# Local attention: the bound on sums of squares as a pairwise maximum, and new step tables for all engines

## The reference, cut to what matters

```python
qkv = x @ Wqkv                       # 16 heads of 64, after a shift of tokens
q = l2norm(q) * qs ; k = l2norm(k) * ksc   # t / max(norm(t), 1e-12)
q = q * cos * scale + rotate_half(q) * sin * scale     # k alike with 1/scale
sim = einsum('bhwie,bhwje->bhwij', bq, bk2) * 8        # window 32, masked
out = einsum('bhwij,bhwje->bhwie', softmax(sim), bv2)
x = x + out @ Wo
```

## Time and profile before

| | us |
|---|---|
| median of 3 runs | 4976.01 (4972.33 to 4977.17) |
| profiled execution, its own time | 4975.52 |
| its span in the trace | 4973.7 |
| busy in the span: PE, DVE, ACT, POOL | 4338.5, 3926.2, 3584.8, 3207.4 |
| first layer's local attention, first product to last normalisation | 584.0 to 1093.6 |

### The profile page before, as it was taken

How to read it: one execution, slowest core, us unless ns; L and a number is a source line. 1 busy time by engine, 2 the same in 40 slices (tenths; PEclk the granted TensorE clock), 3 DMA queues, 4 the chain that set the end, 5 groups by cost and what they waited for, 6 DMA issues and landing times. The chain is left out here.

```text
span 4973.7 us, 153122 instructions
## 1 busy us (share of the span) xinstructions
PE 4338.5 (87%) x50692; PEld 2786.0 (56%) x50694; DVE 3926.2 (79%) x9246; ACT 3584.8 (72%) x13078; POOL 3207.4 (64%) x4057
## 2 busy tenths in 40 slices
PE   6949899988999889998899979998899986676765
PEld 3426566664666646665466645666466664444533
DVE  4779899965999569994899939997499964777488
ACT  5938688874888558884788838887388864777434
POOL 2512399964999569993799928997399962323163
PEclk8969999999999999999999989999899998888886
DMA  2000000000000000000000000000000000000000
GB/s 57 0 19 0 5 2 0 0 18 6 2 0 0 19 7 1 0 0 19 7 0 0 0 24 2 0 0 2 23 2 0 0 18 1 0 0 0 1 26 18
DMA packets 36456, 34.77 MB, mean 7 GB/s; under 512 B 11590, under 2 KB 31300, under 8 KB 35140
## 3 DMA queue, kind: packets, MB, share of 16 engines
q1 hardware_dynamic: 36164, 31.14, 2.1%
HBM read 29.03 MB, written 2.10 MB: 6 GB/s over the span
## 5 line engine op out<-in xcount | busy, mean ns | idle before, releaser
L2477 ACT ACTIVATE local_prob<-ps,local_shift_by 128x128 f32<-128x128 f32 x3072 | 1080.6, 378 | 8.8 <-DVE local_shift_by L2557 8.7
L2405 POOL TENSOR_TENSOR local_qk<-local_qk,local_rsin 128x512 f32<-128x512 f32 x768 | 968.9, 1272 | 61.1 <-DVE local_rsin L2582 61.0
L2716 PE MATMUL ps<-local_wqkv,local_xsT 128*128 128x512 f32 x1536 | 853.2, 642 | 68.4 <-DVE local_rsin L2582 24.9
L2412 POOL TENSOR_TENSOR local_qk<-local_qk,local_inv 128x512 f32<-128x512 f32 x768 | 793.7, 1045 | 174.3 <-ACT local_inv L2496 174.3
L2419 POOL TENSOR_TENSOR local_prob<-local_prob,local_rs 128x512 f32<-128x512 f32 x768 | 791.5, 1042 | 12.6 <-DVE local_rs L2564 12.6
L2477 ACT ACTIVATION_READ_ACCUMULATOR local_prob<-ps,local_shift_by 128x1 f32 x3072 | 670.8, 218 | 0.0
L2571 DVE TENSOR_TENSOR local_qk<-ps,local_cos_t 128x512 f32<-128x512 f32 x768 | 519.7, 677 | 95.0 <-ACT local_sq L2485 90.3
L2485 ACT ACTIVATE local_sq<-ps 128x512 f32<-128x512 f32 x768 | 464.4, 605 | 155.9 <-PE ps L2716 141.9
L2557 DVE TENSOR_REDUCE local_shift_by<-ps 128x4 f32<-128x512 f32 x768 | 524.4, 683 | 63.1 <-PE ps L2792 54.1
L2582 DVE TENSOR_TENSOR local_rsin<-ps,local_sin_t 128x256 f32<-128x256 f32 x1536 | 570.8, 412 | 0.0
L2589 DVE TENSOR_REDUCE local_ss<-local_sq 128x8 f32<-128x512 f32 x768 | 511.4, 667 | 7.8 <-ACT local_sq L2485 7.8
(11 more groups left out here) (331 smaller groups left out, 9174.0 us busy)
## 6 DMA issues: line engine op xcount, KB each, us to landing
local_wqkv<-L_ffn_Wqkv SPq DMA_DIRECT2D x7, 1536.0 KB, 6.8
local_wo<-L_ffn_Wo SPq DMA_DIRECT2D x7, 512.0 KB, 7.3
out<-quantised_res SPq DMA_DIRECT2D x8, 256.0 KB, 2.3
local_w<-L_ffn_W SPq DMA_DIRECT2D x6, 341.0 KB
L_cross_decay<-c_decay SPq DMA_DIRECT2D x1, 1024.0 KB, 11.8
local_w<-L_ffn_W SPq DMA_DIRECT2D x12, 64.0 KB
load_raw<-L_ffn_w SPq DMA_DIRECT2D x8, 64.0 KB, 2.2
local_b<-L_ffn_b SPq DMA_DIRECT2D x24, 0.5 KB
```

Of the source, the lines that this page charges most:

```text
L2405: nc.gpsimd.tensor_tensor(qk[w][:, j, :, :], qk[w][:, j, :, :], rsin[j % 2][:, :, :], ALU.add).then_inc(rot_ready, 1)
L2412: nc.gpsimd.tensor_tensor(qk[w][:, j, :, :], qk[w][:, j, :, :], bcast(inv[:, w, 8 * j:8 * j + 8].unsqueeze(2), [P, 8, LH]), ALU.mult).then ...
L2477: last = nc.scalar.activation(prob[w][:, g, j, :], ps[:, 4 + g % 2, j * P:(j + 1) * P], ACT.Exp, bias=shift_by[:, w, h:h + 1], accum_out=s ...
L2716: nc.tensor.matmul(proj_bank(j), xsT[w][:, :], wqkv[:, 512 * j:512 * j + 512], start=True, stop=True).then_inc(proj_ready, 1)
```

## The change

The sums of squares get a second column per head that holds the constant 1e-24, written once per layer by POOL. The bound is then a `tensor_reduce` that takes the maximum over each pair and writes a new tile `bounded`, where it was a `tensor_scalar` in place. The logarithm reads `bounded`. The four step tables and the one of PE are rewritten, with other leads and lags. Each engine keeps the same calls: the evacuations of DVE are still `evacuate_qk(…, p = 1)`, values half 0 and heads half 1, the others are still ACT's. No wait inside a function is changed.

```diff
-    ss, lnss, inv = (sb(n, [P, 2, 4 * 8]) for n in ("ss", "lnss", "inv"))
+    ss = sb("ss", [P, 2, 4 * 8, 2])
+    bounded, lnss, inv = (sb(n, [P, 2, 4 * 8]) for n in ("bounded", "lnss", "inv"))
...
+            nc.gpsimd.memset(ss[:, :, :, 1:2], 1e-24)
...
-            sequence_loop(pool, NB, 0, 6, step)
+            sequence_loop(pool, NB, 6, 0, step)
...
-                    nc.scalar.activation(lnss[:, w, :], ss[:, w, :], ACT.Ln, scale=2.0 ** 20).then_inc(lnss_ready, 1)
+                    nc.scalar.activation(lnss[:, w, :], bounded[:, w, :], ACT.Ln, scale=2.0 ** 20).then_inc(lnss_ready, 1)
...
-                    nc.vector.tensor_reduce(ss[:, w, 8 * j:8 * j + 8], sq[j % 2][:, :, :], AX, ALU.add).then_inc(ss_summed, 1)
+                    nc.vector.tensor_reduce(ss[:, w, 8 * j:8 * j + 8, 0], sq[j % 2][:, :, :], AX, ALU.add).then_inc(ss_summed, 1)
...
-                    nc.vector.tensor_scalar(ss[:, w, :], ss[:, w, :], 1e-24, None, ALU.max).then_inc(ss_ready, 1)
+                    nc.vector.tensor_reduce(bounded[:, w, :], ss[:, w, :, :], AX, ALU.max).then_inc(ss_ready, 1)
...
-            sequence_loop(dve, NB, 1, 5, step)
+            sequence_loop(dve, NB, 3, 3, step)
...
-            sequence_loop(pe, NB, 0, 5, step)
+            sequence_loop(pe, NB, 0, 6, step)
```

More of the change, by code:

```diff
@@ L2424, in step @@
                 v = 1 - u
[L2425 to L2440, removed]
-            sequence_loop(pool, NB, 0, 6, step)
+                normalise(n + 1, v, 2, live)
+                normalise(n + 1, v, 3, live)
+                to_unit(n + 3, v, 1, live)
+                rotate(n + 4, u, 1, live)
+                to_unit(n + 3, v, 3, live)
+                normalise(n + 2, u, 0, live)
+                normalise(n + 2, u, 1, live)
+                copy_for_values(n + 4, u, live)
+                rotate(n + 4, u, 2, live)
+                keep(n, u, live)
+                fetch(n + 6, u, live)
+                low_half(n, u, live)
+                rotate(n + 4, u, 3, live)
+                to_unit(n + 4, u, 2, live)
+                to_unit(n + 4, u, 0, live)
+                rotate(n + 5, v, 0, live)
+            sequence_loop(pool, NB, 6, 0, step)
         @block.scalar
@@ L2524, in step @@
                 v = 1 - u
-                evacuate_heads(n + 1, v, 0, live)
                 evacuate_x(n + 5, v, live)
+                exponentials(n + 2, u, 2, live)
+                exponentials(n + 2, u, 3, live)
+                high_half(n, u, live)
+                squares(n + 5, v, 0, live)
                 evacuate_qk(n + 3, v, 1, 0, live)
-                exponentials(n + 3, v, 0, live)
-                squares(n + 5, v, 0, live)
+                log_variance(n - 1, v, live)
                 log_norms(n + 4, u, live)
-                high_half(n, u, live)
                 over_norms(n + 4, u, live)
                 squares(n + 5, v, 1, live)
-                exponentials(n + 3, v, 1, live)
                 evacuate_probs(n + 2, u, 0, 1, live)
                 evacuate_probs(n + 2, u, 0, 0, live)
+                exponentials(n + 3, v, 0, live)
+                exponentials(n + 3, v, 1, live)
+                squares(n + 5, v, 2, live)
+                evacuate_qk(n + 4, u, 0, 0, live)
+                evacuate_heads(n + 2, u, 0, live)
                 evacuate_values(n + 3, v, 1, live)
-                log_variance(n - 1, v, live)
-                squares(n + 5, v, 2, live)
                 over_deviation(n - 1, v, live)
[L2541 to L2544, removed]
                 evacuate_probs(n + 2, u, 1, 0, live)
                 evacuate_probs(n + 2, u, 1, 1, live)
+                squares(n + 5, v, 3, live)
             sequence_loop(act, NB, 5, 1, step)
@@ L2640, in step @@
                 v = 1 - u
[L2641 to L2669, removed]
-            sequence_loop(dve, NB, 1, 5, step)
+                maxima(n, u, 2, live)
+                maxima(n, u, 3, live)
+                one_over_sums(n, u, 0, live)
+                one_over_sums(n, u, 1, live)
@@ new lines, in step @@
+                cosines(n + 2, u, 3, live)
+                sines(n + 2, u, 3, live)
+                sums_of_squares(n + 2, u, 2, live)
+                evacuate_values(n + 1, v, 0, live)
+                sums_of_squares(n + 2, u, 3, live)
+                evacuate_qk(n + 1, v, 1, 1, live)
+                evacuate_heads(n - 1, v, 1, live)
+                bound_norms(n + 2, u, live)
+                cosines(n + 3, v, 0, live)
+                sines(n + 3, v, 0, live)
+                maxima(n + 1, v, 0, live)
@@ new lines, in step @@
+                cosines(n + 3, v, 1, live)
+                sines(n + 3, v, 1, live)
+                one_over_sums(n, u, 2, live)
+                one_over_sums(n, u, 3, live)
+                maxima(n + 1, v, 1, live)
+                sums_of_squares(n + 3, v, 0, live)
+                sums_of_squares(n + 3, v, 1, live)
+                statistics(n - 2, u, live)
+                aggregate(n - 2, u, live)
+                residual(n - 1, v, live)
+                evacuate_qk(n + 2, u, 0, 1, live)
@@ L2672, in _ @@
+                cosines(n + 3, v, 2, live)
+                sines(n + 3, v, 2, live)
+                norm(n - 3, v, live)
+            sequence_loop(dve, NB, 3, 3, step)
         @block.tensor
@@ L2872, in step @@
                 v = 1 - u
+                project_values(n - 3, v, 0, live)
+                weighted_values(n - 5, v, 1, live)
+                turn_qk(n - 3, v, 1, live)
+                shift(n - 6, u, live)
+                project(n - 1, v, 0, live)
+                project(n - 1, v, 1, live)
+                scores(n - 3, v, 0, live)
+                turn_probs(n - 4, u, 0, live)
+                output(n - 5, v, live)
+                project_values(n - 3, v, 1, live)
+                project(n - 1, v, 2, live)
                 turn_qk(n - 2, u, 0, live)
-                output(n - 5, v, live)
+                weighted_values(n - 4, u, 0, live)
+                scores(n - 3, v, 1, live)
+                turn_probs(n - 4, u, 1, live)
+                turn_x(n, u, live)
                 project(n - 1, v, 3, live)
[L2876 to L2889, removed]
-            sequence_loop(pe, NB, 0, 5, step)
+            sequence_loop(pe, NB, 0, 6, step)
     ph.close()
```

## The result

The changed kernel takes 4935.1 us, the median of 11 runs (4923.4 to 4961.8), against 4975.1 for the kernel before, also of 11: a ratio of 0.9922 (0.9908 to 0.9937). It is 40 us faster where 84 were forecast. The time lies inside the stated range, but the gain is less than half of the forecast one. It is, to a microsecond, the time of rivals 1 and 3.

What follows compares the result with a forecast made beforehand. It took a closed chain through the held bound to set 15.03 us a block. Loop -8.4, start -5, tail -1 and memset +0.2 give -14.2 a layer, -85 over six layers: 4891 us, range 4840 to 4945.

Steps and rivals of the forecast that it cites:

- rival 1: Loop: POOL stays the limit, still waiting for `inv` after rotate 3; 14.9 us a block, 4936 us; chance 0.15.
- rival 3: DVE's normalisation L2636 is held behind POOL in its new place; about 14.9 us a block, 4936 us; chance 0.05.
- The reduction's price: DVE's new bound instruction in the loop: taken as 0.22 us, between 0.17 and 0.67.
- the hold's 0.9: DVE's loss per block at the old bound, about 0.9 us; only 0.38 us expected back, PE being next.
- rival 2: The reduction bound is held like the scalar form, chain closes again at 15.03; about 4971 us; chance 0.07.
- rival 4: Slower: a chain through ACT's copies and exponentials closes over PE; 15.35 us a block, 5030 us; chance 0.07.
- PE's floor: PE's own work in the loop as the limit left: 14.65 us a block, bounds 14.5 and 14.9.
- my layout: One period of PE's new order laid out from start-to-start distances, from value product 0 to end at 14.6 us.
- the third change of shape: On PE, product 2 before the transposition of queries: costs 0.1 to 0.2 us more.
- Loop: 22 blocks a layer, each from 15.03 to 14.65 us: -8.4 us a layer.
- Start: The 9 blocks from the first bound to the loop: -5 us a layer, ends 0 and -10.
- Tail: From the last bound to the layer's end: -1 us a layer, ends -3 and +2.

Runs made afterwards that it cites:

- the first experiment: The kernel before with the bound as a reduction and its constant column, step tables unchanged: 4872.5 us, ratio 0.9798.
- late-normalisation kernel: The changed kernel with the normalisation moved 1.2 us later in DVE's table, behind the two maxima and ahead of the reciprocals: 4837.8 us, ratio 0.9730.

## Why the prediction was right or wrong

**The kernel before was read rightly.** The bound held behind POOL's rotate closed the chain at 15.03; with the reduction alone the period is 14.46 and PE is full. The reduction's price was taken as 0.22 and measured 0.20. That the hold's 0.9 does not come back whole since PE is next at 14.5 is what the first experiment shows: 0.57 of it came back. POOL's wait for `inv` fell as forecast, and rivals 1, 2 and 4 did not come: in the late-normalisation kernel PE is busy 309.1 of 310 us, so neither POOL nor a wait for exponentials limits it, and the reduction is never held.

**The step that failed is rival 3, and its 0.05.** I wrote that L2636 "took 316 to 347 ns in all 192 cases, beside POOL's work", and took that as evidence against the Trainium skill's rule (SBUF — State Buffer, "Who interferes with whom"), which would have the instruction held. The trace did not show it in the middle of POOL's work. Its row in one block of the kernel before:

```profile
722.81 0.34 DVE L2636 TENSOR_SCALAR XN<-local_xs,local_moments,local_rstd 128x128 f32 x1
```

POOL stood idle then: it waited 0.59 for the residual and began its copy at 723.22, and the normalisation ended at 723.15. So it is in 108 of the 192 cases: POOL is idle when the normalisation starts. In the other 84 a POOL multiplication has 0.07 to 0.21 left, too little to lengthen it. The 192 cases without a hold were a few phases repeated, as an order by hand repeats every phase, and none of them was the one that matters. The new place is in the middle of a rotate, and there the runs show the hold: `tensor_scalar` up to 1.92, a form with two SBUF inputs up to 1.98, `tensor_reduce` 0.29 at most. That section of the Trainium skill has `tensor_scalar` in a two-port mode and an instruction with two SBUF inputs contend with GpSimd, and `tensor_reduce` on trn2 never. The trace agrees on all three forms.

**Rival 3's size.** I priced one POOL instruction, 0.9 us, and 14.9 a block. Measured are 1.9 and 15.3 when a second POOL instruction gets in at the release, 0.9 and 14.3 when not. The mean of 15.0 and the time of 4935 hit the rival's 4936 in part by luck: at its 14.9 the loop would have given -2.9 a layer and gave -0.7, and the start gave -7.2.

**PE's floor: the term was mis-sized.** I took 14.65; the same order measures 14.32 with PE full, and the old one 14.46 where I read 14.5 to 14.59. PE's rows in the late-normalisation kernel, from product 2 on:

```profile
840.64 1.02 PE L2718 MATMUL ps<-local_wqkv,local_xsT 128*128 128x512 f32 x2
841.59 0.71 PE L2764 MATMUL ps<-ident,local_qk 64*128 64x64 f32 x16
842.23 1.09 PE L2845 MATMUL ps<-local_probT,local_vals 128*64 128x128 f32 x16
843.25 0.36 PE L2788 MATMUL ps<-band,identb 64*64 64x256 bf16 x4
844.84 0.33 PE L2693 MATMUL ps<-ident,local_xin 128*128 128x128 f32 x1
845.01 1.02 PE L2718 MATMUL ps<-local_wqkv,local_xsT 128*128 128x512 f32 x2
845.87 1.02 PE L2734 MATMUL ps<-local_wqkv,local_xvT 128*128 128x512 f32 x2
846.82 0.44 PE L2845 MATMUL ps<-local_probT,local_vals 128*64 128x128 f32 x4
```

Product 2 before the transposition of queries costs 0.95 (840.64 to 841.59), where I added 0.1 to 0.2 to 0.86; a value product before weighted values 0.95 (845.87 to 846.82) and not the 1.01 that product 1 cost there before. The transposition of x costs 0.17 (844.84 to 845.01) and not the 0.3 of my layout. And no product stands behind a group of 64 rows or columns of the array any more, which had cost 0.10 twice, by the 0.96 of the earlier trace rows. From start to start, in one block of each, the six products take 5.68 us in the run with the bound alone and 5.49 here; the shift and the transposition of x take 0.39 and 0.44, and the rest is equal within 0.01. I counted the third change of shape and set off too little against it: -0.14 instead of +0.06.

**The sum.** Loop -8.4 a layer forecast, -0.7 measured, and -15.7 (the loops of the late-normalisation kernel, 14.32 a block) where the hold is short. Start -5 forecast, -7.2 measured: this term was right in kind. The second bound follows the first by 13.1 in this layer (13.6 before) and not by 12 or less; the third then follows by 12.4 where it was 15.8, and the blocks behind it take 13.9 to 14.4. Tail -1 forecast, +0.9 measured. The stretch from the first product to the first bound had no term; it measures +0.35. With the hold nearly gone the kernel takes 4837.8, 137 us below the kernel before, where my sum has 84 and its lowest end 4840. Two errors, a hold at 0.05 and a floor 0.33 too high, pulled in opposite directions.

**Left open.** What decides at the release whether POOL or DVE goes first is not settled: in the loops of the changed kernel 90 late releases start 0.43 to 0.50 behind the start of the rotate, and the 36 early ones 0.45 to 0.49. Nor is it what is left of the rotate: with 0.47 to 0.51 left, the tables alone give 132 times the early release, and the normalisation behind the residual, with 0.47 to 0.50 left, 62 times the late one and 6 times the early. The changed kernel's runs also spread over 38 us where those of the late-normalisation kernel spread over 7; that this spread comes from how often each outcome falls is likely by the two periods, but only one trace of each was read.

## What to carry to other kernels

Before trusting that an instruction is never held, look at what the other engine does in its rows. If it is idle or about to finish each time, the timing protects the instruction, and a new order, or only a shorter neighbour, can take that away. When a reorder goes with a change of form, time each by itself: here the form alone was worth 103 us, form and tables together 40, and one call moved by 1.2 us made it 137. A place to try for an instruction that can be held is one where the engine that holds it needs next something that stands behind the held instruction: by the order of the two it cannot get in a second time, and here no case passed 0.58.

## What the runs showed of the hardware that I had not expected

A held DVE instruction can be passed by a second POOL instruction that was queued behind the first: lengths of 1.5 to 1.9 us for 0.34 of work, in 96 of 192 cases of the changed kernel. Whichever POOL instruction it waits for, it ends 0.08 or 0.09 after it. A `scalar_tensor_tensor` with both inputs in SBUF is held like a `tensor_scalar`, 1.95 us in the median, though one input has a step of 0. A reduction of the same 128 columns in the same place is not held at all.
